# Two fused transformer layers on one core: layer 0's maxima on Pool's DMA queue, its output products three units later, layer 1's first key and context weights split in the last expert tiles, the weight-row table next to the slots

## The chip, the cores and the metric

One core of one Trainium2 chip runs the whole program. The metric is the device time of one execution in microseconds (us), from the first to the last instruction with the launch around it. The engines are TensorE (PE), VectorE (DVE), ScalarE (ACT), GpSimd (Pool) and SyncE (SP); SP does no arithmetic and issues DMAs. PE reads its operands from SBUF and writes to eight PSUM banks of 128 x 512 f32; ACT and DVE empty the banks.

## What is computed

```python
x = x + L0_xattn(layernorm(x), ctx, ctx, ...)      # 32 heads of 16, 8 kv heads, softmax over 128 keys
x = x + L0_ffn(layernorm(x), ...)                  # 16 experts, top 4 by sigmoid score, plus a shared expert
x = x + L1_xattn(layernorm(x), ctx, ...)           # 32 heads of 128, 4 kv heads, keys are ctx and x itself
x = x + L1_ffn(layernorm(x), ...)                  # dense 512 x 512 plus top-2 adapters of rank 16
```

`x` and `ctx` are 8 x 128 x 512 f32. In layer 0's FFN each token's four best experts are weighted by their normalised scores; `z = silu(x Wg) * (x Wu)`, and `z Wd` is added in with that weight.

## The kernel before

**Precision.** Each f32 operand is split into a high half (fp32r, written by ACT) and a low half (the difference, written by DVE or Pool), and each product is three matmuls: hi hi, hi lo, lo hi (`three`, `mm_group`, L451). So every weight and every intermediate costs one ACT and one DVE pass ahead of PE.

**Order.** The five engines run five programs written out by hand; nothing is scheduled by a planner. Each instruction waits on semaphores by absolute counts, and an engine's instructions run in the order written, as do an engine's DMA issues. A stalled wait holds back all that stands behind it on its engine. `x`, 8 tiles of 128 tokens, stays in SBUF; `B` = 8 batches, `HB` = 4 (half of them), `KT` = 4.

**Layer 0's attention** (`*_attention0`) is a loop of 64 units, eight to a batch. In step i PE computes the scores of unit i + 14 (L616), the turned scores of unit i + 2 (L631) and the attention of unit i (L644). DVE reduces the scores to maxima (L835). When a batch's eight units are reduced, PE transposes its maxima (L623), ACT and DVE split them into `mT` (L722, L842), and they travel through HBM: `mT` is stored to `m_rows` (L516), and when that has landed it is loaded as four extra rows of the query tile `qst` (L518). The turned scores of the batch wait for this load. SP issues both (`maxima` in `sync_attention0`), between the stores of keys and queries and the loads `keys_in`, `queries_in` of later batches. Batch b's maxima are transposed in step 8b - 6 and first needed in step 8b - 2. The output product of batch b (`project_out`, twelve matmuls with `wo0`) is issued by PE in step 8(b + 1) + LAG_Y - 1, that is 5 steps after the batch's last unit, and DVE adds it to `x` one step later. Its operand `a0T` is normalised and split in the steps before. Pool has the low halves of some weights, the bias adds, and `values_spread`. After its last loads SP zeroes the two HBM buffers `moe` (L1048) from the tile `zeros`.

**Routing** (`vector_shared`) runs beside the shared expert's products. DVE finds each token's four experts (`vector_choice`), from the ranks (`tensor_ranks`) each pair's slot (`vector_slots`), and then one-hot tables `tile_hot` (32 pairs x 3 x 48: token, share high, share low) and `row_hot`. PE's product of the two (`tensor_tokens`, L1356) gives the token and the share of each slot, and DVE writes them (`vector_tokens`). `vector_weight_rows` makes the table by which Pool gathers each tile's expert weights.

**Expert tiles** (`*_experts`). 47 tiles of 128 slots: Pool gathers the tokens (L1526) and the weights (L1516, 1.5 MB, skipped where the previous tile of the stream had the same expert, five buffers `raw`), PE transposes, multiplies, turns `z`, and multiplies down; ACT scales the result into `ys` and Pool scatter-adds it to one of the two buffers `moe` (L1537), odd tiles to `moe1`, even tiles to `moe0`. On PE the down product of a tile is behind the gate-up product of the next, and behind the last tile's gate-up stands layer 1's first key group. `returned` are the two buffers read back (L1063), and `vector_return` adds both to `x`.

**Into layer 1.** Layer 1's weights come as a stream of 256 KB pieces (`weight_stream`): 4 key weights, 4 pieces of the context, 4 value weights, then query and output weights. SP loads piece k into one of three buffers `raw1` when piece k - 3 is split (`sync_weight`); ACT and DVE split them in stream order (`scalar_weight`, `vector_weight`, L1693, L1701). `WEIGHTS_AT` says how many are split in which expert tile. `first_opening` is the order of keys, values, returned rows and normalisation ahead of the first queries: `tensor_keys(0, m)` for m under 4 needs only the context, for m from 4 the normalised `x`.

Of the kernel before, what the change touches and what calls it, by code (L numbers as in the profile page):

```python
# [6 lines left out]
F32 = mybir.dt.float32  # L7
# [154 lines left out]
def layers_kernel(nc, A, out):  # L162
    with ExitStack() as whole:
# [87 lines left out]
        xsT = [pair(f"xsT{i}", [P, KT, P]) for i in range(2)]  # L251
        xnB = pair("xnB", [P, KT, HT])
# [82 lines left out]
        fifth_at = place[0]  # L335
# [3 lines left out]
        raw.append(sb("wf_raw4", [P, 3, 2, CH]))  # L339
        place[0] = w1_end  # L340
# [116 lines left out]
        LAG_Y = 6  # L457
# [5 lines left out]
        def sync_attention0():  # L463
# [50 lines left out]
            def maxima(b):  # L514
                sp.wait_ge(S["m0_lo"], b + 1)
                load(m_rows[b].rearrange("q r t -> r q t"), mT[b % 2][:, :, :].bitcast(F32)).then_inc(S["st_m"], 16)  # L516
                sp.wait_ge(S["st_m"], 16 * (b + 1))
                load(qst[b % RING0][QROWS:QROWS + MROWS, :, :, :].bitcast(F32).rearrange("p k j t -> p (k j t)"),  # L518
                     m_rows[b].rearrange("q (h r) t -> (q h) (r t)", h=2)).then_inc(S[f"ld_m0{b % RING0}"], 16)

# [15 lines left out]
            maxima(0)  # L536
            for b in range(1, B):
                maxima(b)
# [153 lines left out]
        def scalar_attention0():  # L692
            def keys(half):
                act.wait_ge(S["k0_mm"], half + 1)
                act.wait_ge(S["ld_bkv0"], 32)
                nc.scalar.activation(k0T[half][0][:, :], banks.of(("k0", half))[:, :], ACT.Identity,
                                     bias=bk[:, 0:1]).then_inc(S["k0_hi"], 1)
# [8 lines left out]
            def query(half, m):  # L706
                act.wait_ge(S["ld_bqo0"], 32)
                act.wait_ge(S["q0_mm"], half * KT + m + 1)
                if half:
                    act.wait_ge(S["st_q"], 48 * KT)  # L710
                nc.scalar.activation(q0T[0][:, m, :], banks.of(("q0", half, m))[:, :], ACT.Identity,
                                     bias=bq[:, m:m + 1]).then_inc(S["q0_hi"], 1)
# [93 lines left out]
        def vector_attention0():  # L806
            def keys(half):
                dve.wait_ge(S["k0_hi"], half + 1)
# [15 lines left out]
            def query(half, m):  # L824
                dve.wait_ge(S["q0_hi"], half * KT + m + 1)
# [128 lines left out]
        def gpsimd_attention0():  # L954
# [32 lines left out]

            pool.wait_ge(S["ld_consts"], 16)
# [55 lines left out]
        def sync_experts():  # L1044
# [14 lines left out]
            for s in range(2):  # L1059
                sp.wait_ge(S[f"st_moe{s}"], 16 * adds_before(TILES, s))  # L1060
            for q in range(B // 2):
                for s in range(2):
                    load(returned[s][:, 2 * q:2 * q + 2, :],  # L1063
# [1388 lines left out]
```

## Time and profile before

| | |
|---|---|
| three runs | 1342.53 us median, 1341.86 to 1344.42 |
| profiled execution | 1342.44 us, span 1341.1 us |
| mean granted TensorE clock | 0.963 of full |
| PE busy | 1218.0 us, 91% |
| DVE / ACT / Pool busy | 63% / 52% / 29% |
| moved by DMA | 130.74 MB in 73664 packets |
| share of the chain that ended last | PE 70%, DVE 9%, Pool 6%, DMA 5% |

A PE that is 91% busy leaves little but its holes; the times below are us from the span's start. Layer 0's attention runs to about 252, routing and the shared expert to 313, the expert tiles to 557, the way into layer 1 to 622. The idle time printed in brackets behind an instruction is what its engine stood ahead of it, and the name behind the arrow is what ended it.

### The profile page before, as it was taken

What the parts mean: (1) busy time and instruction counts of PE and PEld (TensorE: products, weight loads), DVE (VectorE), ACT (ScalarE), POOL (GpSimd) and SP (SyncE); (2) the same over time, 40 slices, a digit from 0 to 9 for tenths busy, and PEclk for the clock granted to TensorE, in tenths of its full rate; (3) what the DMA queues carried; (4) which work ended last, traced back from release to release, by engine and by line L of the source; (5) the groups of instructions that cost most, each with busy time, mean ns of one, the idle gap of its engine ahead of it and who ended that gap; (6) DMA issues with size and microseconds to landing.
All of it is one profiled execution on the core that took longest, in us unless ns stands there. A gap on an engine that the chain in (4) does not pass through costs nothing.

```text
span 1341.1 us, 16367 instructions
## 1 busy us (share of the span) xinstructions
PE 1218.0 (91%) x5860; PEld 951.4 (71%) x5860; DVE 839.9 (63%) x1549; ACT 690.7 (52%) x1575; POOL 389.7 (29%) x452
## 2 busy tenths in 40 slices
PE   4939877797999999878999999999999999999997
PEld 4725554465667667556888888887788888888865
DVE  5526665676777667555466666676456666667857
ACT  3315445415777777523555555565345555556621
POOL 5310001014777768300223233232012232232300
PEclk8969988898999999879999999999999999999999
DMA  7553413119766975552022122121221221211101
GB/s 246 157 168 75 123 28 143 63 41 359 173 104 148 276 205 101 110 173 71 24 64 63 56 64 60 59 64 48 55 64 58 61 63 41 63 57 47 62 1 63
DMA packets 73664, 130.74 MB, mean 97 GB/s; under 512 B 11024, under 2 KB 30352, under 8 KB 70992
## 3 DMA queue, kind: packets, MB, share of 16 engines
q1 hardware_dynamic: 56288, 81.44, 19.6%
q0 software_dynamic: 17296, 48.26, 14.5%
q8 instruction: 47, 0.77, 0.3%
q14 instruction: 33, 0.27, 0.1%
HBM read 150.63 MB, written 29.36 MB: 134 GB/s over the span
## 4 chain that ended last, share of the span: by engine, by line
PE 70%; DVE 9%; POOL 6%; issue 5%; DMA 5%; ACT 3%; SPq 1%; POOLq 0%; ACTq 0%; DVEq 0%
PE bank L451 53%; PE bank L1914 6%; PE bank L1890 4%; POOL moe L1537 3%; PE bank L644 3%; POOL xs L1526 2%; PE bank L631 1%; DMA xs<-xn_rows,token_in 1%; SPq L491 1%; DMA wf_raw<-in_wffn,weight_row 1%; DMA m_rows<-m0T 1%; POOL wf_raw L1516 1%; PE bank L616 1%; DVE xn L422 1%; PE bank L1214 1%
## 5 line engine op out<-in xcount | busy, mean ns | idle before, releaser
L1882 POOL TENSOR_SCALAR p<-p,mx 128x256 f32<-128x256 f32 x256 | 163.2, 654 | 533.4 <-DVE mx L1876 533.4
L1123 DVE TENSOR_TENSOR wf_lo<-wf_raw,wf_hi 128x512 fp32r<-128x512 f32 x192 | 124.4, 689 | 41.4 <-ACT wf_hi L1117 36.0
L451 PE MATMUL bank<-xnA_hi,w1q_hi 128*128 128x512 f32 x288 | 118.5, 412 | 7.2 <-DVE w1q_lo L1701 3.8
L1868 ACT ACTIVATE p<-bank,mx 128x256 f32<-128x256 f32 x256 | 118.0, 485 | 10.7 <-DVE mx L1858 10.6
L1117 ACT ACTIVATE wf_hi<-wf_raw 128x512 fp32r<-128x512 f32 x192 | 110.1, 625 | 15.2 <-DMA wf_raw<-in_wffn,weight_row 14.3
L451 PE MATMUL bank<-xnA_hi,w1q_lo 128*128 128x512 f32 x288 | 114.7, 398 | 0.0
L451 PE MATMUL bank<-xnA_lo,w1q_hi 128*128 128x512 f32 x288 | 114.2, 396 | 0.0
L1897 ACT ACTIVATE p1T_hi<-bank 128x512 fp32r<-128x512 f32 x128 | 75.1, 596 | 65.7 <-PE bank L1890 65.7
L1822 ACT ACTIVATE q1T_hi<-bank 128x512 fp32r<-128x512 f32 x64 | 38.2, 597 | 132.8 <-PE bank L451 132.8
L451 PE MATMUL bank<-w1o_hi,a1T_hi 128*128 128x512 f32 x256 | 105.2, 411 | 0.1
L1828 DVE TENSOR_TENSOR q1T_lo<-bank,q1T_hi 128x512 fp32r<-128x512 f32 x64 | 44.2, 691 | 94.8 <-ACT q1T_hi L1822 94.8
L451 PE MATMUL bank<-wf_raw,zT 128*128 128x512 f32 x220 | 102.8, 592 | 0.9 <-issue 0.5
L451 PE MATMUL bank<-w1o_hi,a1T_lo 128*128 128x512 f32 x256 | 100.3, 392 | 0.0
L451 PE MATMUL bank<-w1o_lo,a1T_hi 128*128 128x512 f32 x256 | 100.2, 391 | 0.0
L1537 POOL DMA_INDIRECT moe<-ys,token_out x47 | 81.5, 1734 | 37.9 <-ACT ys L1206 26.0
L1947 DVE TENSOR_TENSOR x<-bank,x 128x512 f32<-128x512 f32 x64 | 44.2, 691 | 72.0 <-PE bank L451 71.9
L1516 POOL DMA_INDIRECT wf_raw<-in_wffn,weight_row x47 | 50.3, 1070 | 130.9 <-DVE weight_row L1307 91.3
L1902 DVE TENSOR_TENSOR p1T_lo<-bank,p1T_hi 128x512 fp32r<-128x512 f32 x128 | 86.3, 682 | 0.0
L1854 DVE TENSOR_REDUCE mx<-bank 128x2 f32<-128x512 f32 x128 | 81.6, 678 | 0.0
L451 PE MATMUL bank<-wf_hi,xsT_hi 128*128 128x512 f32 x188 | 78.9, 420 | 0.0
L1890 PE MATMUL bank<-consts,p 128*128 128x128 f32 x512 | 75.5, 273 | 2.1 <-DVE a1T_lo L1925 2.1
L835 DVE TENSOR_REDUCE mx<-bank 128x4 f32<-128x512 f32 x64 | 43.2, 688 | 51.7 <-PE bank L616 51.2
(337 smaller groups left out, 3153.2 us busy)
## 6 DMA issues: line engine op xcount, KB each, us to landing
w_raw<-in_wq SPq DMA_DIRECT2D x64, 256.0 KB
w_raw<-in_wo SPq DMA_DIRECT2D x64, 256.0 KB
q0st<-q_rows SPq DMA_DIRECT2D x8, 768.0 KB, 5.6
moe<-xn SPq DMA_DIRECT2D x2, 2304.0 KB, 10.5
q_rows<-q0T_hi SPq DMA_DIRECT2D x16, 256.0 KB
returned<-moe SPq DMA_DIRECT2D x8, 512.0 KB, 7.5
k0bd<-k_rows SPq DMA_DIRECT2D x16, 192.0 KB, 5.9
x<-in_x SPq DMA_DIRECT2D x8, 256.0 KB, 6.7
```

What stands on the lines that cost most here:

```text
L451: ins = nc.tensor.matmul(ps, a, b, start=(n == 0), stop=(n == len(pairs) - 1))
L1117: nc.scalar.activation(wf[m % 2][0][:, a, c, :], raw[m % STREAMS][:, a, c, :], ACT.Copy).then_inc(S["gu_hi"], 1)
L1123: nc.vector.tensor_tensor(wf[m % 2][1][:, a, c, :], raw[m % STREAMS][:, a, c, :], wf[m % 2][0][:, a, c, :].bitcast(F32), ALU.subtract).the ...
L1516: nc.gpsimd.indirect_dma_start(out=raw[m % STREAMS][:, :, :, :].rearrange("p a b c -> p (a b c)"), out_offset=None, in_=A["wffn"].rearrang ...
L1537: nc.gpsimd.indirect_dma_start(out=moe[j % 2], out_offset=bass.IndirectOffsetOnAxis(ap=token_out[:, at:at + 1], axis=0), in_=ys[j % Y_RING ...
L1854: ins = nc.vector.tensor_reduce(m[:, 2 * n:2 * n + 2], banks.of(("s1", s, n))[:, :].rearrange("p (h k) -> p h k", h=2), AX.X, ALU.max)
L1868: ins = nc.scalar.activation(pr1[s % 2][:, h, :], banks.of(("s1", s, n))[:, hh * 2 * P:(hh + 1) * 2 * P], ACT.Exp, bias=m[:, UH + h:UH + h ...
L1882: ins = nc.gpsimd.tensor_scalar(pr1[s % 2][:, h, :], pr1[s % 2][:, h, :], m[:, 3 * UH + h:3 * UH + h + 1], 1.0, ALU.mult, ALU.mult)
L1890: ins = nc.tensor.transpose(ps[:, h * P:(h + 1) * P], pr1[s % 2][:, h, part * P:(part + 1) * P], ident)
L1897: nc.scalar.activation(p1T[0][:, part, :], banks.of(("t1", s, part))[:, :], ACT.Copy).then_inc(S["p1T_hi"], 1)
L1902: nc.vector.tensor_tensor(p1T[1][:, part, :], banks.of(("t1", s, part))[:, :], p1T[0][:, part, :].bitcast(F32), ALU.subtract).then_inc(S[" ...
L1914: ins = nc.tensor.matmul(ps[:, :], a, c, start=(part == 0 and n == 0), stop=(part == 1 and n == 2))
```

## The change

1. **Layer 0's maxima** are issued by Pool (`maxima` in `gpsimd_attention0`), batch 0 and 1 after the second bias adds, batch b behind `values_spread(b)`; the memset of `zeros` stands behind batch 4's. SP issues none.
2. **LAG_Y** is 9 instead of 6: output products, and DVE's adds of them, three steps later.
3. **Routing.** `vector_weight_rows` stands right behind `vector_z(3)`, ahead of the shares. The two products of `tile_hot` with the shares go from DVE to Pool (`gpsimd_tile_share`), issued behind the first two weight gathers.
4. **The fifth weight buffer** `wf_raw4` lies over `xnB` instead of the place of layer 1's context, and its first load waits for the shared expert's eighth gate-up product.
5. **Layer 1's first eight pieces** are split one to a tile in tiles 38 to 45, where before two each were split in tiles 44 and 45 and four in tile 46. SP loads twelve pieces, not eleven, ahead of the returned rows.
6. **The opening.** Value weights wait for the last down product instead of the last scatters. SP reads back `moe1` for the first half as soon as its scatters have landed, then `moe0`; `vector_return(b, s)` adds one buffer. PE runs the three other context keys and the four context values in one piece and then the transpositions of the normalised rows; the four query weights are split among the second key groups instead of behind them.

The semaphores `k0_hi` and `k1_hi` become one, and `q0_hi` and `q1_hi`; counts follow. The core of the diff:

```diff
         xsT = [pair(f"xsT{i}", [P, KT, P]) for i in range(2)]
+        fifth_at = place[0]
         xnB = pair("xnB", [P, KT, HT])
...
-        LAG_Y = 6
+        LAG_Y = 9
...
-            maxima(0)
             for b in range(1, B):
-                maxima(b)
                 if b + 2 < B:
                     queries_in(b + 2)
...
+            def maxima(b):
+                pool.wait_ge(S["m0_lo"], b + 1)
+                nc.gpsimd.dma_start(m_rows[b].rearrange("q r t -> r q t"), mT[b % 2][:, :, :].bitcast(F32)).then_inc(S["st_m"], 16)
+                pool.wait_ge(S["st_m"], 16 * (b + 1))
+                nc.gpsimd.dma_start(qst[b % RING0][QROWS:QROWS + MROWS, :, :, :].bitcast(F32).rearrange("p k j t -> p (k j t)"),
+                     m_rows[b].rearrange("q (h r) t -> (q h) (r t)", h=2)).then_inc(S[f"ld_m0{b % RING0}"], 16)
...
             out_bias(1)
-            for b in range(2, HB + 2):
+            maxima(0)
+            maxima(1)
+            for b in range(2, B):
                 values_spread(b)
-            pool.wait_ge(S["k0_mm"], 2)
-            pool.wait_ge(S["v0_mm"], B)
-            nc.gpsimd.memset(zeros, 0.0).then_inc(S["vp_set"], 1)
-            for b in range(HB + 2, B):
-                values_spread(b)
+                maxima(b)
+                if b == HB:
+                    pool.wait_ge(S["k0_mm"], 2)
+                    pool.wait_ge(S["v0_mm"], B)
+                    nc.gpsimd.memset(zeros, 0.0).then_inc(S["vp_set"], 1)
...
+            sp.wait_ge(S["st_moe1"], 16 * adds_before(TILES, 1))
+            for q in range(B // 4):
+                bring(1, q, S[f"returned{q}"])
+            sp.wait_ge(S["st_moe0"], 16 * adds_before(TILES, 0))
+            for q in range(B // 4):
+                bring(0, q, S[f"rows_in{q}"])
+            for q in range(B // 4, B // 2):
+                for s in (1, 0):
+                    bring(s, q, S[f"rows_in{q}"])
...
+        def gpsimd_tile_share():
             hot = tile_hot[:, :, :, :].bitcast(F32)
+            for n, (c, part) in enumerate(((1, share_hi), (2, share_lo))):
+                pool.wait_ge(S["tile_hot"], 2 * n + 1)
+                nc.gpsimd.tensor_tensor(
+                    tile_hot[:, :, c, :], hot[:, :, 2, :],
+                    flat(part).bitcast(F32).unsqueeze(2).broadcast_to([P, PAIRS, TILE_COLS]),
+                    ALU.mult).then_inc(S["tile_hot"], 1)
...
             vector_z(3)
+            vector_weight_rows()
             vector_shares()
             vector_tile_token()
...
             vector_z(5)
-            vector_tile_share()
             vector_row_hot()
-            vector_weight_rows()
...
-        WEIGHTS_AT = {TILES - 3: 2, TILES - 2: 2, TILES - 1: KT}
+        WEIGHTS_AT = {j: 1 for j in range(TILES - 2 * KT - 1, TILES - 1)}
...
             weights(2)
+            gpsimd_tile_share()
             pool.wait_ge(S["st_xn"], 32)
...
             gather(3)
+            pool.wait_ge(S["gate_mm"], 2)
+            pool.wait_ge(S["gu_mm"], B)
             weights(4)
...
-        FIRST_LOADS = 2 * KT + 3
+        FIRST_LOADS = 3 * KT
...
             if ring == "out" and slot < 4:
-                for s in range(2):
-                    act.wait_ge(S[f"st_moe{s}"], 16 * adds_before(TILES, s))
+                act.wait_ge(S["dn_mm"], FFN_STEPS)
...
+        def tensor_first_opening():
+            for m in range(1, KV1):
+                tensor_keys(0, m, score_banks)
+            for b in range(HB):
+                tensor_values(0, 0, b, score_banks)
+            for j in range(3, 7):
+                tensor_norm(4, j, out_banks)
+            for m in range(KV1, 2 * KV1):
+                tensor_keys(0, m, score_banks)
...
+        def vector_first_opening():
+            for _ in range(3):
+                vector_weight()
+            vector_keys(0, 0)
+            vector_keys(0, 1)
+            vector_weight()
+            for b in range(HB):
+                vector_return(b, 1)
+            vector_keys(0, 2)
+            vector_keys(0, 3)
+            for j in range(2):
+                vector_return(2 * j, 0)
+                vector_return(2 * j + 1, 0)
+                vector_norm(4, j)
+            vector_norm(4, 2)
+            for b in range(HB):
+                vector_norm(4, b + 3)
+                vector_values(0, 0, b)
+            for m in range(KV1, 2 * KV1):
+                vector_keys(0, m)
+                vector_weight()
+                for s in (1, 0):
+                    vector_return(HB + m - KV1, s)
```

## Rows read from the trace of the kernel before

**Rows 1.** Timeline, PE, 76 to 140: start, length, line, operation; [idle before <-releaser].
```profile
96.34 0.79 PE L631 MATMUL bank<-q0st,k0bd 100*128 100x256 f32 x2 [18.84 <-DMA q0st<-m_rows]
...
103.13 0.27 PE L623 MATMUL bank<-consts,mx 128*32 128x128 f32 x1
...
108.14 0.47 PE L631 MATMUL bank<-q0st,k0bd 100*128 100x256 f32 x2 [0.50 <-DMA q0st<-m_rows]
...
121.13 0.80 PE L451 MATMUL bank<-wo_hi,a0T_hi 128*128 128x512 f32 x1 [2.19 <-DVE a0T_lo L861]
...
138.79 0.47 PE L451 MATMUL bank<-wo_hi,a0T_hi 128*128 128x512 f32 x1 [2.29 <-DVE a0T_lo L861]
```

**Rows 2.** Waits of PE, 100 to 255: total us, times, longest.
```profile
PE bank L451 <- DVE a0T_lo L861: 17.2, 7, 3.8
```

**Rows 3.** Timeline, PE, around the first expert tile.
```profile
283.14 1.45 PE L451 MATMUL bank<-wf_raw,zT 128*128 128x512 f32 x3
...
309.94 1.09 PE L1214 MATMUL bank<-consts,xs 128*128 128x128 f32 x4 [5.83 <-DMA xs<-xn_rows,token_in]
...
312.84 0.78 PE L451 MATMUL bank<-wf_hi,xsT_hi 128*128 128x512 f32 x1
```

**Rows 4.** Waits of PE, 555 to 622.
```profile
PE bank L451 <- DVE w1o_lo L1701: 9.9, 1, 9.9
...
PE bank L451 <- DVE q1T_lo L1701: 5.8, 1, 5.8
...
PE bank L451 <- DVE w1q_lo L1701: 3.3, 1, 3.3
```

**Rows 5.** Busy us by stretch: PE, PEld, DVE, ACT, POOL (instructions), granted clock, DMA.
```profile
509.00:555.00 46.00, 46.00 (x196) 32.18 (x195) 33.70 (x55) 36.19 (x73) 31.57 (x23) 1.00 0.61 103
```

**Rows 6.** Timeline, GpSimd and VectorE, 68 to 76.
```profile
68.44 4.99 POOL L959 TENSOR_TENSOR x<-x,bo 128x512 f32<-128x512 f32 x4
...
75.18 0.27 DVE L842 SCALAR_TENSOR_TENSOR m0T<-bank,m0T 32x128 fp32r<-32x128 f32 x1
```

**Rows 7.** Timeline of the DMAs that SP issues, 84 to 207.
```profile
84.19 1.13 SPq L516 DMA_DIRECT2D m_rows<-m0T  x1
...
93.87 0.27 SPq L518 DMA_DIRECT2D q0st<-m_rows  x1
...
104.05 0.33 SPq L516 DMA_DIRECT2D m_rows<-m0T  x1
...
106.58 0.31 SPq L511 DMA_DIRECT2D q0st<-q_rows  x1
...
206.64 1.03 SPq L1048 DMA_DIRECT2D moe<-xn  x2
```

**Rows 8.** The source line L516, the maxima's stores, issue to landing.
```profile
DMA to landing us min/median/max: 1.4/1.5/9.7
```

**Rows 9.** Timeline, GpSimd and VectorE, 275 to 300.
```profile
298.84 0.97 POOL L1526 DMA_INDIRECT xs<-xn_rows,token_in  x1 [0.30 <-issue]
...
275.41 0.75 DVE L1168 TENSOR_TENSOR z<-bank,silu 128x256 f32<-128x256 f32 x2
...
280.87 1.28 DVE L1197 TENSOR_TENSOR x<-bank,x 128x512 f32<-128x512 f32 x2
...
291.89 0.95 DVE L1296 TENSOR_TENSOR ended<-ends,by_p 128x768 f32<-128x768 f32 x1
...
294.77 0.21 DVE L1307 SCALAR_TENSOR_TENSOR weight_row<-again,tile_f 128x48 uint32<-128x48 f32 x1
```

**Rows 10.** The chain that ended last, 555 to 625: start, us, what.
```profile
563.77 5.04 PE bank L451 x12
...
572.52 4.85 DMA moe<-ys,token_out
...
577.80 4.92 DMA returned<-moe
...
607.15 11.39 PE bank L451 x48
```

More of the change, by code:

```diff
@@ L339, in layers_kernel @@
         raw.append(sb("wf_raw4", [P, 3, 2, CH]))
+        assert place[0] <= fifth_at + 2 * KT * HT * 4
         place[0] = w1_end
@@ L807, in keys @@
             def keys(half):
-                dve.wait_ge(S["k0_hi"], half + 1)
+                dve.wait_ge(S["k_hi"], half + 1)
                 nc.vector.scalar_tensor_tensor(
@@ L1661, in sync_attention1 @@
         def sync_attention1():
-            for k in range(FIRST_LOADS + 1, len(stream)):
+            for k in range(FIRST_LOADS, len(stream)):
                 sync_weight(k)
@@ L1731, in vector_keys @@
                                     k1T[0][:, g, part, :].bitcast(F32), ALU.subtract).then_inc(S["k1_lo"], 1)
-        def first_opening(weight, keys, values, back, norm):
-            for g in range(KV1):
-                keys(0, g)
-                weight()
-                if g % 2:
-                    back(g - 1)
-                    back(g)
-                    norm(4, g // 2)
-            norm(4, 2)
-            for b in range(HB):
-                values(0, b)
-                norm(4, b + 3)
-            for g in range(KV1):
-                keys(0, KV1 + g)
-                back(HB + g)
+        def tensor_first_opening():
+            for m in range(1, KV1):
+                tensor_keys(0, m, score_banks)
+            for b in range(HB):
+                tensor_values(0, 0, b, score_banks)
[3 more added lines that the diff above has]
+                tensor_keys(0, m, score_banks)
@@ new lines, in scalar_first_opening @@
+        def scalar_first_opening():
+            for _ in range(3):
+                scalar_weight()
+            scalar_keys(0, 0)
+            scalar_keys(0, 1)
+            scalar_weight()
+            scalar_keys(0, 2)
+            scalar_keys(0, 3)
+            scalar_values(0, 0, 0)
+            scalar_values(0, 0, 1)
+            scalar_norm(4, 1)
+            scalar_values(0, 0, 2)
+            scalar_values(0, 0, 3)
+            for j in range(3, 7):
+                scalar_norm(4, j)
+            for m in range(KV1, 2 * KV1):
+                scalar_keys(0, m)
+                scalar_weight()
@@ new lines, in vector_first_opening @@
+        def vector_first_opening():
+            for _ in range(3):
+                vector_weight()
[14 more added lines that the diff above has]
+                vector_values(0, 0, b)
+            for m in range(KV1, 2 * KV1):
+                vector_keys(0, m)
+                vector_weight()
+                for s in (1, 0):
+                    vector_return(HB + m - KV1, s)
@@ L1945, in vector_out @@
             else:
-                dve.wait_ge(S["moe_add"], half * HB + b + 1)
+                dve.wait_ge(*returned_all(tile))
             nc.vector.tensor_tensor(x[:, tile, :], banks.of(("y1", s))[:, :], x[:, tile, :],
@@ L1953, in half_steps @@
         def half_steps(half, values, query, weight, steps, norm, last, ending):
-            for b in range(HB):
+            for b in range(HB if half else 0):
                 weight()
-                if half:
-                    values(0, b)
+                values(0, b)
             for n in range(UH):
@@ L1991, in steps @@
                     tensor_attend(s - 1)
[L1994 to L1996 removed]
+            tensor_first_opening()
             for half in range(2):
@@ L2020, in steps @@
                     scalar_attend(s - 1)
-            first_opening(scalar_weight, scalar_keys, lambda part, b: scalar_values(0, part, b), nothing, scalar_norm)
+            scalar_first_opening()
             for half in range(2):
```

79 lines of the change are left out of this document (34 added, 45 removed).

## The prediction

> **What bounds the kernel now.** I read the slices of the page first, then the chain of waits stage by stage, then the timelines around its gaps. TensorE (PE) is busy for 91% of the span, so only its holes, and the stretches in which it runs at half clock behind a hole, can be saved. Four stages of the change have such holes. (a) PE stands 18.84 us before the first turned scores of layer 0 [rows 1]. (b) In layer 0's steady part PE waits seven times for the low half of a0T ahead of an output product, 17.2 us in all [rows 2]. (c) Between routing and the first expert tile it waits 5.83 us for the gathered tokens [rows 3]. (d) Between the last expert tile and layer 1's queries it waits 5.8, 9.9 and 3.3 us for weight splits [rows 4]. In the expert tiles themselves PE has no hole: 46.00 us busy of 46.00, with VectorE (DVE) at 33.7 and ScalarE (ACT) at 36.2 [rows 5].
>
> **(a) The first maxima.** Batch 0's maxima are complete at 75.45 (75.18 + 0.27), and GpSimd (Pool) is free from 73.43 [rows 6]. SyncE (SP) issues their store only at 84.19, after its twelve query stores; the store lands when the reload is issued, at 93.87, and PE starts at 96.34 [rows 1, 7]. The median of the eight such stores is 1.5 us [rows 8], so 8 of its 9.7 us are queueing. On Pool the store goes out at 75.5 in a queue of its own, while SP's stores still fill the transfer engines. No row shows a direct transfer on Pool's queue. Bounds: SP's undisturbed round trip of store and reload, 4.1 us (104.05 to 108.14) [rows 1, 7], and both legs at the worst landing seen, 9.7 + 2.5. I take 7: two issues of about 0.97 each (what a Pool issue costs [rows 9]) in place of SP's 0.3, plus a share for full engines. PE then starts at 82.5 to 83 instead of 96.34, **-13 us**, bounds -16 and -7. The Trainium skill, "DMA: Bandwidth & Descriptors", section "Issuing engines are not separate DMA queues", speaks against this: it says another issuing engine saves only sequencer time. Its section "Queues, rings and completion order" says each transfer engine alternates between queue rows, which would let the small store past. The 9.7 against 1.5 us shows only that one queue's order is kept; it cannot choose between them.
>
> **(b) The steady part of layer 0.** Output products go three units later. A unit of scores, turned scores and attention is some 1.3 us of PE (three and a half of them take 4.5, below), so 4 us of other work lies before the product, and waits of about 2.2 us vanish; the largest, 3.8, nearly does. The last batch's wait stays (nothing is left to put before it): about 15.3 us removed. But that product stood between the maxima's transposition and the turned scores that need them. With it gone the trip has only four units: from 103.13, PE was ready at 107.64 (108.14 - 0.50), which is 4.5 us [rows 1]. The transposed maxima are split 1.0 us after it, so SP's trip of 4.1 us just misses (0.5 us). Pool's trip is 5.8 by the issue costs above: 1.0 + 5.8 - 4.5 = 2.3 us of new hole in batches 1 to 7. The reload also meets SP's 768 KB of queries, which go out when the previous batch's turned scores end (106.58 [rows 7]), no longer behind it in one queue: I take 2.6. SP, freed of maxima, reaches its zero fill (now 206.64 [rows 7]) some 13 units earlier, inside batch 6's trip: 5 us there. Sum 5 x 2.6 + 5 + 2.3 = 20.3 against 15.3 + 0.5 removed: **+5 us**. The half clock seen behind a 2.2 us hole (the first product takes 0.80 us at 121.13 and 0.47 at 138.79, behind holes of 2.19 and 2.29 [rows 1]) I leave as often as before. Bounds of the trip: 4.1 us leaves 0.5 us holes, -12 and up to 10 more off for half clock; 8 us gives holes of 4.5, +16. Pool's queue holds the value spreads and the zero memset behind these waits; they were ready a whole batch ahead and stay hidden. The Trainium skill, same page, section "Anatomy of one DMA — SWDGE (gpsimd) path", gives about 2.0 us fixed for each; by it the trip would be about 4 and this term -12.
>
> **(c) Routing.** DVE builds the weight-row table last, 291.9 to 295.0, and Pool then issues 3 MB of expert weights; the first gather goes out at 298.84 behind them and PE gets its rows at 309.94, wants the third down product's bank at 283.14, and starts the first tile's products at 312.84 [rows 3, 9]. The table (3.1 us of DVE) moves behind the z products that end at 276.1, so the weights are issued at 279.3 and landed before the gather. Two products over 1536 elements leave DVE for Pool. Pool does 512 elements in 1.25 us [rows 6], so 1536 take 3.8 each: 282.2 to 290, before the token product at 292.5; they cost nothing unless Pool is twice as slow. The shared adds (0.64 each) come 3.1 us later: the first ended at 281.5, now 284.8, so that bank is late by 1.7. Tokens are therefore known 1 us later (297.9), the gather lands near 302, and PE, which has its own work until 305.8, goes to the first gate-up product at 307.8 instead of 312.84, without the half clock behind the present hole (1.3 us): **-6 us**, bounds -8 and -2. The fifth weight buffer waits for the eighth gate-up product, over before the tokens: nothing.
>
> **(d) Into layer 1.** The eight key and context splits go one to a tile in the last tiles, 0.6 us of ACT and 0.7 of DVE in 5.15. Before, two a tile already fitted with PE full [rows 5]; cost nothing, bound +2. What they free: PE's first key group no longer waits 5.8 us or runs at half clock (5.04 against 2.85 us a group, 11.39 / 4 [rows 10]), so it ends at 560.4, not 568.8. The last tile's transposition and down product are queued behind that group. Its scatter moves from 572.52 to 564.2, lands 4.85 later at 569, and the rows come back 4.92 later [rows 10] near 574 instead of 582.7. The other stream's rows come earlier and are added before. PE meanwhile has three key and four value groups, 7 x 2.85 = 20 us, and ends them at 582. DVE after 574: four adds (0.64 each, as the shared adds [rows 9]), four statistics, square root and reciprocal, an estimate of 7.5 us; then four rounds of scale, turn and split, an estimate of 2 us each, to 589.5. Context rows are thus no longer the hole; the normalisation is, 7.5 us, with half clock behind it (+1.8). The second key groups start at 589.5 instead of 607.15: -17.6 + 1.8 = **-16 us**. In those groups DVE does a key split, a weight split and two adds, 2.75 us in 2.85: it just fits, and the four query weights are ready when the queries begin. The 3.3 us wait there goes: **-3 us**. Bounds of both together -23 and -12.
>
> **Sum.** -13 + 5 - 6 - 16 - 3 = -33 us against the profiled execution: 1342.4 (span 1341.1 and 1.3 around it), which is the median of the three runs (1342.5) to 0.1. **1309 us.** Layer 1 behind the queries is PE-bound and unchanged.
>
> **Rivals.**
> 1. Pool's trip is as short as SP's (4.1 us): holes of 0.5 us, PE stays at full clock. (b) is -12 to -22 instead of +5: about 1290. For it: the small size; against: a Pool issue is three times SP's. Chance 0.18.
> 2. The first store on Pool gains nothing since full engines serve it no sooner than now, or the trips take 8 us: (a) 0 and (b) +5, or (a) -10 and (b) +16. About 1322. For it: the transfer row full there and the queries in the way. Chance 0.2.
> 3. Pool's trip decides against the change: every store or reload shares engines with queries, keys and zero fill, and takes a whole landing as bad as 9.7 us beside 2.5. Holes are 1.0 + 12.2 - 4.5 = 8.7 us, seven of them 61 against 15.8, (a) -8: 1342 + 45 - 8 - 25 = 1354. It decides from a trip of about 11.5 us on. Against it: the median of the eight stores is 1.5 us beside SP's traffic, and only the first, in the full queue, took 9.7 [rows 8]. Chance 0.04.
> 4. The opening does not do what it says: DVE blocks on the returned rows ahead of two key splits, PE's banks wait, and only 9 of 19 us come: 1319. Chance 0.12.
> Forecast 0.46.
>
> **Numbers.** The range, 1288 to 1325, takes in the forecast, most of rivals 1, 2 and 4. Faster by over 0.2% (2.7 us, about what a measurement tells from none) 0.94, within 0.02, slower 0.04.
>
> **What would show it.** First turned scores at 82 to 84, with a wait on the reload of 4 to 5 us instead of 18.8. No wait on a0T's low half but the last; instead waits of 2 to 3 us on the reload in each batch (rival 1: 0.5; rival 3: 8), the largest in batch 6. First expert weights issued near 16 us before the token gather, gather waits gone. No hole before layer 1's first keys; one hole of 5 to 8 us on the normalised rows; none before the queries. Wrong would be: DVE late in the key groups, PE waits inside the last eight tiles, or a hole before the token product from Pool's shares.

## The result, and the profile after

| | before | after |
|---|---|---|
| median of the runs shown together | 1342.19 us (4 runs) | 1322.03 us (4 runs, 1319.94 to 1322.55) |
| profiled execution, its span | 1342.44, 1341.1 | 1322.04, 1320.6 |
| mean granted TensorE clock | 0.963 | 0.970 |

The ratio is 0.9846, 95% interval 0.9828 to 0.9864. The forecast was 1309 with 1288 to 1325 around it, so the direction and the range held, but 13.0 of the 33.4 us expected against the profiled execution did not come. The stages tell where. Each row below is the start of a PE instruction that both kernels have.

| PE reaches | before | after | difference | of it in this stage | forecast |
|---|---|---|---|---|---|
| first turned scores of layer 0 | 96.34 | 89.00 | -7.3 | -7.3 | -13 |
| first product of the shared expert | 252.47 | 256.46 | +4.0 | +11.3 | +5 |
| first gate-up product of the expert tiles | 312.84 | 311.60 | -1.2 | -5.2 | -6 |
| second key groups of layer 1 | 607.15 | 588.72 | -18.4 | -17.2 | -16 |
| the end of the span | 1341.1 | 1320.6 | -20.5 | -2.1 | -3 |

Routing and the way into layer 1 came out to within 1.5 us each. The whole miss lies in layer 0. These are the holes of PE there, from the timeline after (start, length, line, operation, and the idle time before it with what ended it); the first answers to [rows 1], and L623 is what L631 was.

```profile
89.00 0.80 PE L623 MATMUL bank<-q0st,k0bd 100*128 100x256 f32 x2 [11.43 <-DMA q0st<-m_rows]
104.02 0.47 PE L623 MATMUL bank<-q0st,k0bd 100*128 100x256 f32 x2 [3.27 <-DMA q0st<-m_rows]
120.23 0.47 PE L623 MATMUL bank<-q0st,k0bd 100*128 100x256 f32 x2 [3.52 <-DMA q0st<-m_rows]
141.55 0.76 PE L623 MATMUL bank<-q0st,k0bd 100*128 100x256 f32 x2 [5.49 <-DMA q0st<-m_rows]
162.58 0.77 PE L623 MATMUL bank<-q0st,k0bd 100*128 100x256 f32 x2 [4.97 <-DMA q0st<-m_rows]
183.41 0.77 PE L623 MATMUL bank<-q0st,k0bd 100*128 100x256 f32 x2 [5.03 <-DMA q0st<-m_rows]
```

Those of batches 6 and 7 are 1.85 and 2.94, so that the seven behind the first come to 27.1 us. The waits of PE in layer 0 after (total, times, longest) show what they replaced: of the 17.2 us on the low half of a0T [rows 2] only the last batch's remains.

```profile
PE bank L623 <- DMA q0st<-m_rows: 38.5, 8, 11.4
PE bank L452 <- DVE a0T_lo L853: 2.9, 1, 2.9
```

Why the holes are that long is in the chain of waits after (start, us, what; 76 to 218). A trip is a store of 32 KB and a reload. The store takes 1.8 to 2.1 us to land in each batch but the first; the reload 4.4 to 6.3 while queries are under way (batches 1 to 5), and 2.9 and 2.8 in batches 6 and 7, where none are left.

```profile
76.00 6.37 DMA m_rows<-m0T
82.66 6.29 DMA q0st<-m_rows
...
97.42 1.81 DMA m_rows<-m0T
99.51 4.38 DMA q0st<-m_rows
...
133.07 1.78 DMA m_rows<-m0T
135.13 6.28 DMA q0st<-m_rows
...
217.46 2.76 DMA q0st<-m_rows
```

SP's side of the same moments (timeline, the DMAs that SP issues): its query load goes out 0.2 us after Pool's reload at 99.51, and 0.4 before the one at 135.13. Before, the reload stood ahead of the load in one queue: the load went out 2.5 us after the store [rows 7], which is 1.0 us after the reload's issue at 105.53.

```profile
99.69 0.31 SPq L512 DMA_DIRECT2D q0st<-q_rows  x1
...
134.75 0.30 SPq L512 DMA_DIRECT2D q0st<-q_rows  x1
```

In routing, DVE's row table, Pool's weights and its two share products after; the gather that stood behind the weights [rows 9] is issued at 302.8, and no PE wait on gathered rows is left where [rows 3] had 5.83 us.

```profile
284.11 1.15 POOL L1522 DMA_INDIRECT wf_raw<-in_wffn,weight_row  x1 [62.09 <-DVE weight_row L1312]
...
287.06 3.50 POOL L1343 TENSOR_TENSOR tile_hot<-tile_hot,share_hi 128x1536 fp32r<-128x1536 f32 x1
290.64 6.84 POOL L1343 TENSOR_TENSOR tile_hot<-tile_hot,share_lo 128x1536 fp32r<-128x1536 f32 x1
...
289.71 5.13 DVE L1353 TENSOR_TENSOR row_hot<-at_row,rows_of 128x4096 fp32r<-128x4096 f32 x1
```

Into layer 1, PE's timeline after has only these waits between 559 and 625. The 5.8, 9.9 and 3.3 us of [rows 4] are gone; four waits on the normalised rows take 1.2, 2.1, 1.0 and 1.5.

```profile
581.29 1.07 PE L432 MATMUL bank<-consts,xn 128*128 128x128 f32 x8 [1.21 <-DVE xn L423]
584.48 0.63 PE L432 MATMUL bank<-consts,xn 128*128 128x128 f32 x4 [2.12 <-DVE xn L423]
586.12 1.09 PE L432 MATMUL bank<-consts,xn 128*128 128x128 f32 x4 [1.02 <-DVE xn L423]
588.72 0.77 PE L452 MATMUL bank<-xnA_hi,w1q_hi 128*128 128x512 f32 x1 [1.50 <-DVE xnA_lo L446]
```

### The profile page after: what moved, and what is told of

Read it like the earlier page. It is cut to its first block, busy times and chain, and to the rows that moved or that the text cites. A ratio compares the mean times of both kernels' runs of the same rounds, so it can differ in the third digit from the quotient of the medians.

```text
span 1320.6 us, 16364 instructions
## 1 busy us (share of the span) xinstructions
PE 1217.0 (92%) x5860; PEld 950.2 (72%) x5860; DVE 836.3 (63%) x1547; ACT 691.5 (52%) x1575; POOL 410.1 (31%) x470
## 4 chain that ended last, share of the span: by engine, by line
PE 70%; DVE 9%; DMA 7%; issue 6%; POOL 5%; ACT 3%; SPq 0%; POOLq 0%; DVEq 0%; ACTq 0%
PE bank L452 52%; PE bank L1967 6%; PE bank L1943 4%; DMA q0st<-m_rows 3%; POOL moe L1543 3%; PE bank L636 3%; POOL xs L1532 2%; DMA m_rows<-m0T 1%; PE bank L2282 1%; PE bank L623 1%; DVE rden L842 1%; DMA wf_raw<-in_wffn,weight_row 1%; DVE xn L423 1%; PE bank L432 1%; PE bank L1219 1%
## 5 line engine op out<-in xcount | busy, mean ns | idle before, releaser
L723 ACT ACTIVATE p<-bank 128x512 f32<-128x512 f32 x64 | 37.8, 594 | 77.4 <-PE bank L623 77.4
```

## The experiments

Two theories stood against each other for layer 0. A: the trips are long because Pool now issues them at the same time as SP issues its queries (and, for the first, its stores), where SP's own order had kept them apart. B: they cost this much by any queue once the output product no longer stands in front of the turned scores, or Pool's queue is slow in itself. All medians are of four runs, each beside the kernel before on the same chip (1341.9 to 1343.4). Unless another kernel is named, each edit is made to the changed kernel.

### All maxima on SP, products nine units behind

The first part is SP's program, the second Pool's.

```diff
             for m in range(KT):
                 queries_out(1, m)
+            maxima(0)
             for b in range(1, B):
+                maxima(b)
                 if b + 2 < B:
                     queries_in(b + 2)
...
             out_bias(1)
-            maxima(0)
-            maxima(1)
             for b in range(2, B):
                 values_spread(b)
-                maxima(b)
```

> The changed kernel, with all eight maxima trips back on SP in their old places (the first behind the twelve query stores, the others ahead of the next batch's query load in the same queue); output products stay three units later. Theory A (the long reloads of the changed kernel come from the 768 KB of queries that SP now issues in the same moment, not from Pool's queue as such): SP's trip is the 4.1 us seen before, holes of batches 1 to 7 shrink from 27.1 us together to about 7 x 0.5 = 3.5, and the first turned scores go back from 89.0 to 96.3: 1322.0 - 23.6 + 7.3 = about 1306 us. Rival B (once the output product no longer covers the trip, it costs this much by any queue): holes stay at 27, first scores at 96.3, about 1329 us.

1301.22 us, ratio 0.9687 (0.9671 to 0.9704): 20.8 us faster than the changed kernel. PE's timeline has the first scores late again and the holes behind them small.

```profile
97.15 0.80 PE L632 MATMUL bank<-q0st,k0bd 100*128 100x256 f32 x2 [19.21 <-DMA q0st<-m_rows]
108.96 0.48 PE L632 MATMUL bank<-q0st,k0bd 100*128 100x256 f32 x2 [0.49 <-DMA q0st<-m_rows]
...
150.67 0.47 PE L632 MATMUL bank<-q0st,k0bd 100*128 100x256 f32 x2 [0.73 <-DMA q0st<-m_rows]
```

Its chain shows the trip, store 1.46 and reload 2.48, and the timeline of SP's issues shows that the query load goes out while the reload is still under way (0.5 us behind it in batch 4, whose reload takes 2.38).

```profile
104.86 1.46 DMA m_rows<-m0T
106.34 2.48 DMA q0st<-m_rows
```

```profile
148.16 0.26 SPq L519 DMA_DIRECT2D q0st<-m_rows  x1
148.65 0.33 SPq L512 DMA_DIRECT2D q0st<-q_rows  x1
```

Theory B's first half, that it costs this much by any queue, falls. The run beat A's 1306 by 5 us. PE's waits on reloads fell by 12.5 us, where A had 16.3, and what more than made up for it is PE's clock: between 76 and the end of the stage these are busy us and instructions of the changed kernel, then of this one (columns: stretch, its length, PE busy (instructions), granted clock, DMA share, GB/s).

```profile
76.00:256.00 180.00, 133.07 (x495) 0.86 0.31 95
```

```profile
76.00:236.00 160.00, 124.05 (x495) 0.89 0.34 107
```

Idle time falls by 11.0 us, 46.93 to 35.95, and the same number of instructions (495) takes 9.0 less. Behind a 4.97 us hole the changed kernel starts at the lower of the two levels (1.2 GHz, 0.77 for the first pair of turned scores and 1.91 for the pair of context products); here, behind a hole of 0.73, the same pairs take 0.47 and 1.02, the upper level.

```profile
162.58 0.77 PE L623 MATMUL bank<-q0st,k0bd 100*128 100x256 f32 x2 [4.97 <-DMA q0st<-m_rows]
163.15 1.91 PE L636 MATMUL bank<-p,v0p 128*128 128x512 f32 x2
...
167.60 0.80 PE L452 MATMUL bank<-wo_hi,a0T_hi 128*128 128x512 f32 x1
```

```profile
150.98 1.02 PE L645 MATMUL bank<-p,v0p 128*128 128x512 f32 x2
...
154.24 0.80 PE L452 MATMUL bank<-wo_hi,a0T_hi 128*128 128x512 f32 x1
```

From the turned scores to the output product that is 5.0 us against 3.6: this hole costs 1.4 us more than its length. The granted clock of the 5 us behind a hole shows the same for the others, in the columns from above: 0.50 to 0.67 behind each of the changed kernel's seven holes of 1.85 to 5.49 us, here those of batches 1 and 6,

```profile
104.02:109.02 5.00, 5.00 (x15) 0.66 0.47 83
203.11:208.11 5.00, 5.00 (x15) 0.66 0.00 0
```

and 1.00 in this run behind those of batches 1 to 5 (0.49 to 1.25 us), here batch 4.

```profile
150.67:155.67 5.00, 5.00 (x21) 1.00 1.15 272
```

### Queries wait for the reload

```diff
             for b in range(1, B):
+                sp.wait_ge(S[f"ld_m0{b % RING0}"], 16 * (b // RING0 + 1))
                 if b + 2 < B:
                     queries_in(b + 2)
```

> The changed kernel, with one wait added on SP: the load of the queries two batches on is issued only when the maxima of the present batch have come back on Pool's queue. Theory A (the reloads of batches 1 to 5, 4.4 to 6.3 us, are long because the queries go out in the same moment): they fall to the 2.8 us of batches 6 and 7, where no queries are in flight; the holes shrink by 1.6, 1.7, 3.5, 3.0 and 3.0, together 12.8 us: about 1309 us. Rival B (Pool's queue is slow in itself, whatever SP does): 1322, unchanged.

1305.61 us, ratio 0.9733 (0.9710 to 0.9756). Nothing was moved off Pool, SP only waits longer, and 16.4 us come back. The chain has the reload at 2.8:

```profile
126.69 1.78 DMA m_rows<-m0T
128.75 2.82 DMA q0st<-m_rows
```

The holes are 1.66, 1.61, 2.03, 1.98 and 2.05 in batches 1 to 5. So A holds, and the second half of B, that Pool's queue is slow in itself, falls but for a small part: SP's loads beside it make the reload 1.6 to 3.5 us longer. The edit holds back all that SP issues behind the wait, so that it doesn't tell the 768 KB of queries from what follows them at once: two key loads of 192 KB in batches 1 to 4, the shared expert's weights in batch 4, the zero fill in batch 5. What is left between Pool and SP with neither disturbed is 0.8 to 1.3 us of hole a batch (1.6 to 2.1 against 0.5 to 1.3).

The Trainium skill says in "DMA: Bandwidth & Descriptors", section "Issuing engines are not separate DMA queues", that transfers started by different engines run interleaved on the same sixteen transfer engines and that a second issuing engine saves only sequencer time. These reloads agree, 4.4 to 6.3 us beside the queries and 2.8 without. The price of giving up the common queue is in the runs: on SP, with the query load issued 0.5 to 1.1 us behind it and before it had landed, the reload took 2.4 to 2.9 us; on Pool, with the query load issued between 0.4 us ahead and 0.2 us behind, 4.4 to 6.3. No run has the two in different queues with SP's head start, so that the order within one queue is not told apart from that head start.

### The two edits of layer 0 apart

```diff
-        LAG_Y = 9
+        LAG_Y = 6
```

The first of two runs has this edit alone, with maxima on Pool; the second has it with maxima on SP in their old places, so that layer 0 is as before and only routing and the opening are changed.

> The changed kernel with the output products of layer 0 back in their old place, three units earlier; maxima stay on Pool. Theory A (the product, 2.9 us, and the wait ahead of it covered the trip): the waits on the reload of batches 1 to 7, 27.1 us, vanish but for 0 to 3 us in the longest trips, and the waits on a0T's low half come back with 15.8 us: about 1311 us, so that moving the products three units on costs 11 us when Pool carries the maxima. Rival (the reload's queue, not the cover, makes the hole): holes of 2 to 4 us stay on the reload beside those on a0T, about 1322 or more.

1313.57 us, ratio 0.9783 (0.9766 to 0.9799). The waits of PE there: seven on a0T's low half again, and of the reloads only the first and one of 3.2 us.

```profile
PE bank L452 <- DVE a0T_lo L853: 17.2, 7, 3.9
PE bank L623 <- DMA q0st<-m_rows: 13.8, 2, 10.6
```

> The changed kernel with both edits of layer 0 undone: maxima on SP in their old places, output products at their old distance; routing and the way into layer 1 stay changed. Theory A (the parts add up): layer 0's attention ends 4.0 us earlier than in the changed kernel, 252.5 instead of 256.5: 1322.0 - 4.0 = about 1318 us. With it the four combinations of queue and distance stand side by side (Pool and SP, six and nine units), and the rest of the change (routing and opening) is worth 24.4 us by itself. Rival: the later stages take back part of what layer 0 gives, and it ends above 1320.

1316.82 us, ratio 0.9806 (0.9777 to 0.9835). The four combinations, with the start of the shared expert's first product in brackets:

| | products 6 units behind | 9 units behind |
|---|---|---|
| maxima on SP | 1316.8 (252.8) | 1301.2 (236.8) |
| maxima on Pool | 1313.6 (250.4) | 1322.0 (256.5) |

Each edit alone gains, 15.6 us the later products and 3.2 us Pool (the 95% intervals of these two runs overlap, so that 3.2 is hardly clear of noise; the stage ended 2.3 earlier in the profiles); both together lose 5.2. Later products take away the work that hid the trip, and Pool makes the trip longer, so each sets what the other is worth.

### Products eleven units behind

```diff
-        LAG_Y = 9
+        LAG_Y = 11
```

> The changed kernel with one number changed: output products eleven units behind instead of nine, which by the loop's order puts each product again right behind a maxima transposition, between it and the turned scores that wait for the trip, and still five units after its own inputs. Maxima stay on Pool. Theory A (the hole is trip minus cover, and the product of 2.9 us is cover): the seven reload waits of 3.3, 3.5, 5.5, 5.0, 5.0, 1.9 and 2.9 us fall by 2.9 each, to about 8 us in all, and no wait on a0T's low half comes back but the last: 1322 - 19 = about 1303 us. Rival (the product only moves the wait, since the split of the maxima on ScalarE and VectorE then also comes later): above 1312.

1306.55 us, ratio 0.9727 (0.9711 to 0.9744), 3.5 above A's figure. The holes ahead of the turned scores are 10.47, 3.36 and 3.77 us in batches 0 to 2, and there is none in batches 3 to 5, where PE waited 5 us before. Batch 6 has one of 3.91: its store, issued at 172.67, took 5.39 us to land, after SP had issued the zero fill from 162.24 to 165.9. Eleven units behind, the first product comes in batch 3's trip; in batches 1 and 2 there is none to cover it, which I had not seen. So the reload waits behind the first come to 11.0 us, not 8, and other waits grew: 3.0 us new on ScalarE's exponentials, 1.0 more on a0T's low half, 1.7 more on the normalised rows. In batch 3 the product did more than cover: SP's query load went out 2.9 us behind the reload (134.65 against 131.78), not 0.4 ahead of it. How much of the 5 us was cover and how much a shorter trip, this run doesn't tell.

### Where the first trip goes

SP waits here until the first maxima are back before it issues the second half's stores (three of keys, twelve of queries); the query loads wait as above.

```diff
             queries_in(2)
+            sp.wait_ge(S["ld_m00"], 16)
             keys_out(1)
```

> The run in which the query loads wait for the maxima's return on Pool's queue, with one wait more: SP holds the second half's key and query stores back until batch 0's maxima have come back. Theory A (the first trip's two legs of 6.4 and 6.3 us on Pool were the transfer engines full of these stores): the legs fall to 1.8 and 2.8 us, the first turned scores start at about 81 instead of 88.4; batch 1's trip now meets the stores and takes as long as the first did, a hole of about 9 us instead of 1.7, so the sum stays near 1305.6 us (1303 to 1308). Rival B (a transfer on Pool's queue takes 6 us the first time, whatever the engines do): first turned scores still at 88.4, and about 1305 to 1312 us.

1306.21 us, ratio 0.9725 (0.9709 to 0.9742). PE and the chain:

```profile
81.70 0.80 PE L625 MATMUL bank<-q0st,k0bd 100*128 100x256 f32 x2 [4.00 <-DMA q0st<-m_rows]
102.41 0.76 PE L625 MATMUL bank<-q0st,k0bd 100*128 100x256 f32 x2 [9.50 <-DMA q0st<-m_rows]
```

```profile
76.26 2.02 DMA m_rows<-m0T
78.59 3.07 DMA q0st<-m_rows
...
89.58 5.38 DMA m_rows<-m0T
95.23 7.04 DMA q0st<-m_rows
```

The two legs of 6.4 and 6.3 us in the changed kernel came from the second half's key and query stores under way; with these held back they are 2.0 and 3.1, and the same stores then lengthen batch 1's legs to 5.4 and 7.0. Pool's first use of its queue is not the cause.

The next three kernels have the maxima on SP and change only SP's order. First, batch 0's trip ahead of the second half's stores:

```diff
             queries_in(2)
+            maxima(0)
             keys_out(1)
```

> As the run with all maxima on SP, but the first trip stands in SP's order right behind the third query load, ahead of the second half's key and query stores, so that nothing of that half is queued before it. Theory A (the first trip's 12.7 us on Pool were full transfer engines, filled by the twelve query stores): with these held back both legs are short, 4 to 5 us from 75.5, and the first turned scores start at 80 to 81 instead of 89.0 (Pool) or 96.3 (SP, old place); the other holes as in that run: about 1290 us, 16 below it. Rival: the legs stay at 6 us each because of the loads already in flight, scores at 89, about 1298; or the query stores, now 5 us later, hold up a later batch and give it back, about 1295 to 1300.

1295.78 us, ratio 0.9666 (0.9647 to 0.9685). The first turned scores start at 79.98, as A said, but batch 1's at 103.24 behind a hole of 11.78: its store stood in SP's order behind all of the others, was issued at 95.19 and took 5.4 us to land. Then batch 1's trip and batch 3's queries ahead of the stores as well:

```diff
             queries_in(2)
+            maxima(0)
+            maxima(1)
+            queries_in(3)
             keys_out(1)
```

> As the run with the first trip early on SP, but batch 1's trip and batch 3's query load also stand ahead of the second half's key and query stores. Theory A (batch 1's 11.8 us hole there was its store waiting in SP's order behind the twelve query stores, not slow engines): that hole falls to 0.5 to 1 us, and the stores, issued some 12 us later, are still done long before batch 4 asks for the second half's queries: 1295.8 - 11 = about 1285 us. Rival: the queries of batch 4 and its keys are now late and batch 4 waits as much: about 1295.

1302.25 us, ratio 0.9710 (0.9682 to 0.9738): a miss of 17 us. Batch 1's hole is 0.43, and batch 2 has one of 15.65.

```profile
92.59 0.47 PE L635 MATMUL bank<-q0st,k0bd 100*128 100x256 f32 x2 [0.43 <-DMA q0st<-m_rows]
119.27 0.77 PE L635 MATMUL bank<-q0st,k0bd 100*128 100x256 f32 x2 [15.65 <-DMA q0st<-m_rows]
```

I had asked only when the stored queries are read, not which trip comes up while SP issues them. SP issues stores from 91.5 to 109.5 and keys to 111.4, longer than the some 11 us between two trips. So they were split over two gaps:

```diff
+            maxima(0)
             keys_out(1)
-            for m in range(KT):
-                queries_out(1, m)
+            queries_out(1, 0)
+            queries_out(1, 1)
+            maxima(1)
+            queries_in(3)
+            queries_out(1, 2)
+            queries_out(1, 3)
+            keys_in(4)
```

> Maxima on SP, products nine units behind. In SP's order the trip of batch 0 stands ahead of the second half's stores, the key stores and half of the query stores (six of twelve) stand between it and the trip of batch 1, the other half behind that trip and ahead of batch 2's. Theory A (what a trip pays is what is queued ahead of it in SP's order: 11.8 us in batch 1 with all stores behind trip 0, 15.7 us in batch 2 with all behind trip 1): some 9 us of issuing fit into the 11 us between two trips, so that holes stay at 0.5 to 1.5 us: about 1285 us, 11 below the run with the first trip early. Rival (the transfers themselves, still under way when the next trip starts, hold it): holes of 4 to 5 us in batches 1 and 2, about 1292.

1291.88 us, ratio 0.9621 (0.9605 to 0.9638). The rival's figure of 1292 is the one that came: batch 1 still has a hole of 4.70 us, for its store, issued at 88.4, landed 5.3 later behind the nine stores (three of keys, six of queries) that SP had issued since 78.2. But batch 2, where the rival had one of 4 to 5 too, has 0.99; batches 3 to 6 have 0.9 to 1.1, and batch 7 has 2.1. Last, this order with products eleven units behind:

> As the run with the stores spread over two gaps, with output products eleven units behind instead of nine. Theory A: the remaining holes ahead of the turned scores, 0.5 to 1.3 us in each of seven batches, are covered by the product, and a store still under way has 2.9 us more: 5 to 8 us below that run, about 1279 us. Rival: the holes were no longer bound by the trip, 1285, the same.

1289.35 us, ratio 0.9591 (0.9575 to 0.9607), 2.5 below, not 5 to 8. The four runs, 1287.3 to 1294.0, overlap with the 1291.4 to 1294.4 before, so that a gain is not shown. The holes of batches 3 and later are gone as expected (the reload waits fall from 13.9 to 7.8 us), but three waits elsewhere grew: on a0T's low half of the last batch 3.9 us instead of 2.9, on the normalised rows 2.8 instead of 1.4, and 3.2 us new on ScalarE's exponentials. In the two profiles the stage took the same time from the first turned scores on, 146.8 us.

### Routing and the opening

Layer 0 as before, and routing undone too, so that only the last tiles and the opening of layer 1 are changed (and the place of the fifth weight buffer, which stays):

```diff
-            vector_weight_rows()
             vector_shares()
...
+            vector_tile_share()
             vector_row_hot()
+            vector_weight_rows()
```

> As the run with layer 0 as before, but routing is also put back: the two share products on VectorE, the weight-row table behind the row table, expert weights issued after it. Only the last tiles and the opening of layer 1 are then changed. Theory A (d is worth 19 to 20 us and c 5, and they add): 1342.4 - 19.5 = about 1323 us, 5 above that run. Rival: the late weights and gather reach nothing once the tiles run, or d needs the earlier routing: 1318 or 1328.

1323.45 us, ratio 0.9859 (0.9837 to 0.9882). That is 18.4 us under before for the opening, and 6.6 above the run with routing changed. The trace has the gather wait back, and the stage from the shared expert to the first tile takes 60.2 us again against 55.2. In the changed kernel's stages the two came to 19.3 and 5.2, so the parts add.

```profile
311.05 1.08 PE L1225 MATMUL bank<-consts,xs 128*128 128x128 f32 x4 [5.78 <-DMA xs<-xn_rows,token_in]
```

Then the changed kernel with only the share products back on VectorE, the table and the weights early:

```diff
             vector_z(5)
+            vector_tile_share()
             vector_row_hot()
```

> The changed kernel with the two share products (1536 elements a row each) on VectorE again, 1.75 us each, ahead of the row table; the weight-row table and the expert weights stay early. Theory A (the gain of routing, 5 us, comes from the early weights; Pool's shares only moved work, for Pool took 6.8 us over the second one and VectorE's row table 5.1 instead of 4.4 beside it): the row table ends at 297.6 instead of 294.8, still before the token product at 298.0, and the next shared adds come up to 3 us later, which costs at most one wait of 1 to 2 us: 1322 to 1324 us. Rival B (the shares off VectorE carry the gain): about 1326 us.

1318.14 us, ratio 0.9815 (0.9792 to 0.9838), not slower; the stage takes 55.2 us as in the changed kernel. VectorE's timeline:

```profile
288.70 1.75 DVE L1343 TENSOR_TENSOR tile_hot<-tile_hot,share_hi 128x1536 fp32r<-128x1536 f32 x1
290.48 1.76 DVE L1343 TENSOR_TENSOR tile_hot<-tile_hot,share_lo 128x1536 fp32r<-128x1536 f32 x1
292.16 4.42 DVE L1353 TENSOR_TENSOR row_hot<-at_row,rows_of 128x4096 fp32r<-128x4096 f32 x1
```

All of it ends at 296.6, and PE is through with its own gate-up products and starts the token product at 297.05. The shares on Pool moved work that nobody waited for. I don't know what makes this run 3.9 us faster than the changed one, or whether all of it is real: the 95% intervals of the two ratios overlap, and 1.1 us were there before this stage begins, in layer 0, where the two kernels are the same.

## Why the prediction was right or wrong

The range held by routing and the opening. Of layer 0's two edits the forecast expected a gain of 8 us; they cost 4.0 in the stages, and 5.2 against the run with layer 0 as before. There the mechanism was wrong, and that the sum stayed in the range is in part luck.

**(a), -13, measured -7.3.** The step that failed is the trip of 7 us, "two issues of about 0.97 each ... plus a share for full engines". The issues were dearer in the estimate than in fact (a direct transfer takes Pool 0.53 to 0.58 us after a first one of 0.80), but the share for full engines was under 2 us (7 less 4.1 and two issues dearer by 0.67) and measured 7.5: the trip took 12.9 us, 76.00 to 88.95, against 5.4 with the stores held back. The bound of 9.7 + 2.5 = 12.2 us, which gave -7, is what came: it took the transfer engines to be as full as for the landing that it was read from.

**(b), +5, measured +11.3.** The 15.8 us removed were right, but the last batch's wait grew by 1 us to 2.9. Of the new holes, forecast at 20.3 and measured at 27.1, Pool's undisturbed trip was estimated well: hole 2.3 forecast, 1.6 to 2.1 measured where queries wait. (Its 5.8 us don't follow from the issue costs: 4.1 + 2 x 0.67 is 5.4, a hole of 1.9.) The failing step is the one that put 0.3 us on the queries ("no longer behind it in one queue: I take 2.6"): they, and the loads that follow them, cost 1.6 to 3.5. The zero fill met batch 5's reload instead of batch 6's, whose hole was 1.85 for 5. Left out was that PE's waits on the normalised rows fell, from 6.9 to 3.3 us, with the later products. The second failing step is "I leave as often as before" for the half clock. In the 5 us behind the seven product waits before the granted clock was 0.66 to 0.71 six times and 1.00 once; behind the seven new holes it is 0.50 to 0.67 each time, and three of these are longer than any before. From the first turned scores to the end of the stage PE's idle time grew by 7.5 us (27.9 to 35.4) and its busy time by 3.8 (128.2 to 132.0) with one instruction more in the trace, together the 11.3. With (a), idle time was traded one for one (46.9 to 47.0 from 76 on), and nearly all of the +4.0 at the end of the stage are instructions at the lower clock.

**(c), -6, measured -5.2.** Right in the table and the early weights. Pool's shares cost nothing, as said, but with less room: the second took 6.84 us, not 3.8, and ended at 297.48, and PE, at work until then, came to the token product at 298.04. That they gained nothing either was not seen. The Trainium skill's "SBUF — State Buffer", section "Who interferes with whom", says that VectorE and GpSimd share a pair of ports under an exclusive lock, and that a VectorE instruction with two inputs in SBUF contends with a GpSimd instruction that reads SBUF. The rows agree in direction: Pool's product takes 3.50 us beside VectorE's short ones and 6.84 beside the row table, and the table 5.13 instead of 4.42.

**(d), -16 and -3, measured -17.2 and -2.1.** Right, by its own steps: the rows' return at 570.6 where "near 574" was said, and the normalisation the next hole, with 5.9 us in four waits where 7.5 was said. Two sizes were off against each other: the scatter went out at 559.46, not 564.2, and the return took 6.41 us, not 4.92, with its loads issued together.

**The rivals.** The one that the first trip gains less and later trips take about 8 us, 1322, is the one that came in time, though the first trip did gain 7 and the holes were 27, not 31. Rival 1, a trip on Pool as short as SP's with holes of 0.5 us, did not come even with the query loads held back: holes of 1.6 to 2.1 and 1305.6 us, nearer to the forecast's 1309 than to its 1290. The rival on the slower side did not come: the first trip took 12.9 us, but the seven later ones at most 8.3 (133.07 to 141.4), short of the 11.5 from which it decides.

## What to carry to other kernels

The small transfer that an engine waits for stayed short here in two ways: issued ahead of the large ones in the queue that it shares with them, or with the large ones held back until it had landed. Before it goes to an idle queue, ask what the busy queue issues in the next few microseconds, not only what stands ahead in it. When an edit takes away a wait by moving work later, list what that work covered in its old place; here two edits, one with a clear gain and one with a small one alone, lost together, which only the four combinations show.

## What the runs showed of the hardware

- A 32 KB store or reload on Pool's direct queue costs little more than on SP's: 1.79 and 2.77 us to land against 1.46 and 2.48, and 0.55 us of issuing against 0.3.
- Pool's queue does get past stores that SP has queued, in part: with the stores under way, the first turned scores started at 89.0 by Pool and 97.2 behind the stores in SP's order, and batch 1's hole, with the first trip early, was 9.5 us by Pool and 11.8 by SP.
- The clock after a wait on the reload, as the granted clock of the 5 us behind it: in all the runs it was 0.50 to 0.69 behind every one of 2.9 us and more, and 1.00 behind those under 1.7 us but for two (1.09 and 1.11, both 0.66). In between it went either way, 1.00 behind 2.05 and 0.66 behind 2.03 in one run. The output product waits of the kernel before do the same: 0.67 behind 2.19, 1.00 behind 2.29 [rows 1]. The length of such a hole alone does not say which level follows.
- The level can fall a pair of matmuls late: behind the hole of 3.27 the first pair of turned scores took 0.47 us, as at the upper level, and the 5 us as a whole had 0.66.
